# Three passes of a graph network kernel: rings of eight groups and resident indices in the score and harmonic passes, and TensorE's part of them as loops

## The chip, the cores and the metric

The kernel runs on one core of one Trainium2 chip. The metric is the device time of one launch in microseconds (us). The engines are called PE (TensorE, with its weight loads as PEld), DVE (VectorE), ACT (ScalarE), POOL (GpSimd) and SP (SyncE).

## What is computed

The reference is four graph layers on 12,500 nodes with 32 features and 200,000 edges, sorted by target node. Each layer adds its result to x. The parts that matter here, cut down:

```python
h = relu(layernorm(x)); x = x + gcn(h)          # three graph convolutions
h = relu(layernorm(x))                          # attention
q, k, v = h @ Wq, h @ Wk, h @ Wv
scores = einsum('ehd,ehd->eh', q[dst], k[src]) / sqrt(8)
e = exp(scores - segment_max(scores, dst)[dst])
x = x + (segment_sum(e * v[src], dst) / segment_sum(e, dst)) @ Wo
h = relu(layernorm(x)); x = x + relational(h)   # a gated sum over edges with 86 edge types
h = relu(layernorm(x))                          # spherical harmonics (9 numbers sh an edge)
x = x + segment_sum(W * cg * sh * h[src], dst)
```

## The kernel before

Edges are cut into steps of 128 edges, one to a partition, padded so that a step touches one tile of 128 nodes. There are S = 1664 steps. A group is G = 8 steps, so a pass has GROUPS = 208 groups; R = 4 and ITERS = 52 (4 x 52 = 208). Three passes are touched.

Each engine has its own program, and semaphores order them. In all three passes GpSimd gathers the rows of the source nodes from a table in HBM, one indirect DMA a step, eight a group, into a slot of a ring of R = 4 groups. It takes its row numbers from `staged`, into which VectorE copies the group's eight columns of the resident table `k["src"]` (`_stage`, L712). `_gather_rows` (L717, gathers recorded as L725) is the GpSimd program of the relation and harmonic passes; the score pass has its own copy of it (L1818). Before each group GpSimd waits for that group's index copy and for the slot to be free.

**Score pass** (`score_pass`, L1790). SP loads a group's target numbers as rows, broadcast over the partitions (L599). VectorE turns them into a transposed one-hot (`_one_hot_of_rows`, L604), one group ahead. TensorE multiplies the one-hot with the query table, eight matmuls a group (L1859), into `q_edge`, two groups deep in PSUM, which gives each edge its query. VectorE multiplies that with the gathered keys (L1840, two instructions a group), reduces to scores (L1845), and makes the index copy for the group three ahead (L714). SP copies the gathered slot to `dram["kv"]` for a later pass (L1873); it waits for the same gather as the product. A slot is free when the product has read it and the copy to `kv` has landed.

**Relation pass** (`relation_pass`, L2179). Works in half groups: VectorE makes three one-hots (L593, L604), then logits from looked-up rows, then the 2048-wide message (L2241). After the first half of each group it makes the index copy of the group three ahead. TensorE looks rows up (L2254, L2256) and adds messages into node tiles (L640). A one-hot of a half group waits for the look-up of the half after it and for earlier sums. At the end of the pass GpSimd gathers one more group and 98 tiles of `current`.

**Harmonic pass** (`harmonic_pass`, L2416). VectorE makes a group's one-hot (L593), copies its factors to PSUM (L2441), forms the messages (L2472, L2475) and makes the index copy. TensorE adds them into the node tile's sum (L640), and each matmul that ends a step counts `added` up. One-hot and message have two buffers: group n's one-hot waits until the sums of group n - 2 are counted. ScalarE takes finished tiles out (L668, L671).

In these three passes all programs except ScalarE's and the store of tiles are written out in full: the Python loops `for i in range(ITERS)` repeat the instructions 52 times. Elsewhere loops run on the engines (`Fori`): in the attention's value pass (`value_pass`, L2045), which reads `kv` back with plain DMAs and has no gathers, and in the three convolution sums, whose gathers are L1186, whose matmuls are L1261, and whose VectorE part starts with L1268.

## Time and profile before

| what | value |
|---|---|
| median of three runs | 18507.44 us |
| lowest and highest | 18477.56, 18517.64 us |
| span of the profiled execution | 18371.9 us |
| median above the profiled span | 135.5 us |
| GpSimd busy | 9678.5 us, 53% of the span |
| TensorE matmuls busy | 6824.2 us, 37% |
| VectorE busy | 6310.2 us, 34% |
| mean granted TensorE clock | 0.621 of full speed |

The profiled execution has no time of its own besides its span, so the table gives its distance to the median. Busy shares are averages over stages with different limits. The score pass runs from 8196 to 10600 us of the span, the relation pass from 11627 to 15240, the harmonic pass from 15605 to 18189. In the timelines a first number is the start, a second the length, and the brackets give the idle time of the engine before it and what the profile takes for its end; where the engine or transfer named there had long been done, it was another wait of the same instruction.

### The profile page before, as it was taken

How to read it: one execution, taken by the hardware profiler on the slowest of the kernel's cores; microseconds unless marked ns; L12 is line 12 of the kernel's file. 1: busy time of each engine (PE TensorE's matmuls, PEld its weight loads, DVE VectorE, ACT ScalarE, POOL GpSimd, SP SyncE). 2: the span in 40 equal slices, each digit the busy share in tenths (PEclk: the TensorE clock that was granted, in tenths of full speed). 3: DMA queues.
4: the chain of work that ended last, by engine and by line, in shares of the span. 5: the costliest groups of instructions: out<-in, count | busy, mean ns of one | idle time of the engine just before them, and what ended most of it. 6: DMA issues, size and time to landing. Idle time of an engine off the chain costs nothing. (4 is left out here: it accounts for less than half of the span.)

```text
span 18371.9 us, 155481 instructions
## 1 busy us (share of the span) xinstructions
PE 6824.2 (37%) x35336; PEld 4347.2 (24%) x35337; DVE 6310.2 (34%) x14818; ACT 2619.3 (14%) x4127; POOL 9678.5 (53%) x10318
## 2 busy tenths in 40 slices
PE   4122223444442122121111134566666666333335
PEld 1111112222221111110000023233333325333324
DVE  6222222222222333332222276455555541222222
ACT  1112223444442111110000000000000001000001
POOL 0566665555555666646666623344444441656663
PEclk9555555666665555555555555788888875666666
DMA  2111112222221111122222212222222222111111
GB/s 79 28 25 26 25 25 50 58 59 60 61 59 27 19 20 20 19 77 69 66 71 70 66 54 75 46 51 50 52 52 51 52 46 67 19 19 19 19 19 44
DMA packets 756927, 831.33 MB, mean 45 GB/s; under 512 B 348199, under 2 KB 521618, under 8 KB 753655
## 3 DMA queue, kind: packets, MB, share of 16 engines
q0 software_dynamic: 340624, 383.65, 11.4%
q1 hardware_dynamic: 267022, 300.82, 5.6%
q10 hardware_dynamic: 148312, 136.41, 2.7%
q8 instruction: 307, 5.03, 0.1%
q14 instruction: 662, 5.42, 0.1%
HBM read 658.55 MB, written 158.81 MB: 44 GB/s over the span
## 5 line engine op out<-in xcount | busy, mean ns | idle before, releaser
L725 POOL DMA_INDIRECT rel_ring<-scratch_tab,rel_staged x1664 | 1569.9, 943 | 1948.4 <-DVE rel_staged L714 1468.1
L640 PE MATMUL rel_accumulator<-rel_message,rel_onehot 128*128 128x512 f32 x3328 | 1998.0, 755 | 866.1 <-DVE rel_message L2241 818.7
L725 POOL DMA_INDIRECT sh_ring<-scratch_tab,sh_staged x1664 | 1569.8, 943 | 1318.6 <-DVE sh_staged L714 816.7
L1186 POOL DMA_INDIRECT sum1g_ring<-scratch_parts,sum1g_staged x1568 | 1548.3, 987 | 1163.4 <-SPq L1210 662.3
L1186 POOL DMA_INDIRECT sum0g_ring<-scratch_parts,sum0g_staged x1568 | 1539.8, 982 | 1166.3 <-issue 830.8
L1818 POOL DMA_INDIRECT score_ring<-scratch_tab,score_staged x1664 | 1571.9, 945 | 867.7 <-issue 516.9
L1186 POOL DMA_INDIRECT sum2g_ring<-scratch_parts,sum2g_staged x1568 | 1504.7, 960 | 945.8 <-issue 463.9
L640 PE MATMUL sh_accumulator<-sh_message,sh_onehot 128*128 128x248 f32 x3328 | 972.8, 461 | 1662.4 <-DVE sh_message L2475 1369.9
L640 PEld LDWEIGHTS sh_accumulator<-sh_message,sh_onehot 128*128 128x128 f32 x3328 | 788.9, 242 | 1845.7 <-issue 1726.1
L640 PEld LDWEIGHTS rel_accumulator<-rel_message,rel_onehot 128*128 128x128 f32 x3328 | 773.3, 245 | 1772.0 <-issue 1765.2
L1247 ACT COPY sum1g_rows<-sum1g_ring 128x6144 bf16 x196 | 1041.8, 5316 | 357.3 <-issue 315.8
L1859 PE MATMUL score_q_edge<-query_parts,score_onehot_t 128*128 x1664 | 256.4, 259 | 2158.0 <-DVE score_onehot_t L604 1453.5
L2241 DVE TENSOR_TENSOR rel_message<-numbers,rel_ring 128x2048 f32<-128x2048 f32 x416 | 953.3, 2292 | 14.3
L1261 PE MATMUL sum1g_totals<-sum1g_rows,sum1g_onehot 128*128 128x384 bf16 x3136 | 865.0, 456 | 195.9 <-ACT sum1g_rows L1247 155.7
L593 DVE TENSOR_TENSOR rel_onehot<-numbers,k_drel 128x512 f32<-128x512 f32 x419 | 288.2, 688 | 1761.8 <-DMA value_ring<-scratch_kv 1171.1
L593 DVE TENSOR_TENSOR sh_onehot<-numbers,k_drel 128x1024 f32<-128x1024 f32 x208 | 254.4, 1223 | 1801.1 <-DMA rlo_lin_chunk<-scratch_totals 1587.1
L1840 DVE TENSOR_TENSOR score_product<-score_q_edge,score_ring 128x384 f32<-128x384 f32 x416 | 212.2, 552 | 1883.2 <-DMA scratch_type_rows<-table_type_row 631.2
L1268 DVE TENSOR_REDUCE sum1g_joined<-sum1g_totals 128x128 f32<-128x384 f32 x196 | 109.3, 558 | 1969.5 <-remote 1302.2
L1859 PEld LDWEIGHTS score_q_edge<-query_parts,score_onehot_t 128*128 128x128 bf16 x1664 | 173.1, 104 | 2241.4 <-issue 2192.8
L1261 PE MATMUL sum0g_totals<-sum0g_rows,sum0g_onehot 128*128 128x98 bf16 x3136 | 308.2, 282 | 881.3 <-ACT sum0g_rows L1247 444.2
L1319 DVE TENSOR_TENSOR gcn_last<-gcn_last,sum0g_totals 128x2 f32 x196 | 30.1, 154 | 1725.6 <-remote 1536.2
L1261 PEld LDWEIGHTS sum1g_totals<-sum1g_rows,sum1g_onehot 128*128 128x128 bf16 x3136 | 497.4, 165 | 511.8 <-issue 469.2
(417 smaller groups left out, 12414.6 us busy)
## 6 DMA issues: line engine op xcount, KB each, us to landing
score_rows<-scratch_rel_rows SPq DMA_DIRECT2D x211, 256.0 KB
rel_rel_rows<-scratch_rel_rows ACTq DMA_DIRECT2D x211, 256.0 KB
scratch_kv<-score_ring SPq DMA_DIRECT2D x208, 256.0 KB
value_ring<-scratch_kv SPq DMA_DIRECT2D x208, 256.0 KB
rel_type_rows<-scratch_type_rows ACTq DMA_DIRECT2D x211, 172.0 KB
rel_ring<-scratch_tab,rel_staged POOLq DMA_INDIRECT x1672
score_ring<-scratch_tab,score_staged POOLq DMA_INDIRECT x1664
sh_ring<-scratch_tab,sh_staged POOLq DMA_INDIRECT x1664
```

Of the source, the lines that this page charges most:

```text
L593: return nc.vector.tensor_tensor(out[:], k["numbers"][:, 0:P].unsqueeze(1).to_broadcast([P, n, P]), k["drel"][:, bass.ds(first, n)].unsque ...
L640: self.nc.tensor.matmul(self.accumulator[:, bass.ds(self.banks[g], self.width)], onehot, rows, start=False, stop=True, skip_group_check=Tr ...
L725: nc.gpsimd.indirect_dma_start(out=ring[:, q, g, :], out_offset=None, in_=table, in_offset=bass.IndirectOffsetOnAxis(ap=staged[:, q, g:g + ...
L1186: nc.gpsimd.indirect_dma_start(out=ring[:, q % slots, g, :], out_offset=None, in_=table, in_offset=bass.IndirectOffsetOnAxis(ap=staged[:, ...
L1247: self.nc.scalar.copy(self.rows[q % 2][:, :, 0:3 * self.width], self.ring[:, bass.ds(slot, 1), :, :].rearrange("p o g w -> p (o g) w")).th ...
L1261: last = self.nc.tensor.matmul(self.totals[:, q % 2, 0:self.held], self.onehot[q % 2][:, :, g], self.rows[q % 2][:, g, :], start=(g == 0), ...
L1268: self.nc.vector.tensor_reduce(self.joined[q % 2][:], self.totals[:, q % 2, 0:3 * self.width].rearrange("p (c f) -> p f c", c=3), axis=AX_ ...
L1319: nc.vector.tensor_tensor(marks, marks, got.totals[:, q % 2, 3 * D:3 * D + 2], ALU.add)
L1818: nc.gpsimd.indirect_dma_start(out=ring[:, q, g, :], out_offset=None, in_=dram["tab64"][0:J * P, :], in_offset=bass.IndirectOffsetOnAxis(a ...
L1840: last = nc.vector.tensor_tensor(product[q % 2][:, tiles, :].rearrange("p g (c f) -> p g c f", f=D), q_edge[:, q % 2, b, 0:HALF_G * W].rea ...
L1859: last = nc.tensor.matmul(q_edge[:, q % 2, g // HALF_G, at:at + W], onehot_t[q % 2][:, g * P:(g + 1) * P], q_nodes[:, bass.ds(tiles[g] * W ...
L2241: nc.vector.tensor_tensor(message[m % 2][:].rearrange("p g (b f) -> p g b f", f=D), coef[:, m % 2, :, :].unsqueeze(3).to_broadcast([P, H, ...
```

## The change

1. `_stage` goes. Gathers of all three passes take their row numbers straight from `k["src"]`. GpSimd's program waits only for the slot (`slot_waits`); in the relation pass for `messaged`, and the extra group at its end waits for `messaged` too.
2. The rings of the score and harmonic passes have DEEP = 8 groups. The relation pass keeps four.
3. Score: three one-hots and three `q_edge` places instead of two. VectorE makes one-hots two groups ahead instead of one. SP loads rows four ahead.
4. Harmonic: four one-hots and four messages instead of two; group n's one-hot waits for the sums of group n - 4.
5. TensorE's programs of these two passes are loops: six groups a turn, 33 turns, with the first six and the last four groups written out (score); four groups a turn, 52 turns (harmonic). VectorE, GpSimd and SP stay written out.

```diff
-def _stage(nc, k, staged, group, slot):
-    return nc.vector.tensor_copy(staged[:, slot, :], k["src"][:, bass.ds(group * G, G)])
+def _gather_rows(nc, pool, k, table, ring, slots, gathered, slot_waits):
+    for n in range(GROUPS):
+        q = n % slots
+        slot_waits(n, q)
+        for g in range(G):
+            nc.gpsimd.indirect_dma_start(
+                out=ring[:, q, g, :], out_offset=None, in_=table,
+                in_offset=bass.IndirectOffsetOnAxis(ap=k["src"][:, n * G + g:n * G + g + 1], axis=0)).then_inc(gathered[q], DMA)
...
 def score_pass(nc, k, dram, q_nodes, score):
-        ring = sb("ring", [P, R, G, 2 * D])
+        ring = sb("ring", [P, DEEP, G, 2 * D])
-        onehot_t = [sb(f"onehot_t{h}", [P, G * P], BF16) for h in range(2)]
+        onehot_t = [sb(f"onehot_t{h}", [P, G * P], BF16) for h in range(3)]
-        q_edge = psum("q_edge", [P, 2, 2, BANK])
+        q_edge = psum("q_edge", [P, 3, 2, BANK])
+        def slot_waits(pool, n, q):
+            if n >= DEEP:
+                pool.wait_ge(used, n - DEEP + 1)
+                pool.wait_ge(spilled[q], n // DEEP * DMA)
+        def make_one_hot(dve, n):
+            dve.wait_ge(rowed[n % R], (n // R + 1) * DMA)
+            if n >= 3:
+                dve.wait_ge(looked_up, n - 2)
+            _one_hot_of_rows(nc, k, onehot_t[n % 3][:], rows[:, n % R, :]).then_inc(made, 1)
...
+                for n in range(GROUPS):
+                    if n + 2 < GROUPS:
+                        make_one_hot(dve, n + 2)
+                    dve.wait_ge(looked_up, n + 1)
+                    dve.wait_ge(gathered[n % DEEP], (n // DEEP + 1) * G * DMA)
...
             def _(pe):
+                def look_up(n, q):
+                    tiles = _tiles_of(nc, k, n)
+                    pe.wait_ge(made, n + 1)
+                    if not isinstance(n, int) or n >= 3:
+                        pe.wait_ge(used, n - 2)
...
+                for n in range(6):
+                    look_up(n, n)
+                with pe.Fori(0, GROUPS // 6 - 1) as i:
+                    for q in range(6):
+                        look_up(i * 6 + (q + 6), q)
+                for n in range(GROUPS // 6 * 6, GROUPS):
+                    look_up(n, n)
...
 def relation_pass(nc, k, dram, y_nodes, relations, current):
-                _gather_rows(nc, pool, dram["tab64"][0:J * P, :], staged, ring, indexed, released, gathered,
-                             lambda i, q: pool.wait_ge(messaged, (i * R + q) * 2 + 1))
-                pool.wait_ge(indexed, GROUPS + 1)
+                _gather_rows(nc, pool, k, dram["tab64"][0:J * P, :], ring, R, gathered,
+                             lambda n, q: pool.wait_ge(messaged, n * 2 + 1))
+                pool.wait_ge(messaged, GROUPS * 2 + 1)
...
 def harmonic_pass(nc, k, dram):
-        ring = sb("ring", [P, R, G, D])
+        ring = sb("ring", [P, DEEP, G, D])
-        onehot = [sb(f"onehot{h}", [P, G, P]) for h in range(2)]
-        message = [sb(f"message{h}", [P, G, SH_WIDTH]) for h in range(2)]
+        onehot = [sb(f"onehot{h}", [P, G, P]) for h in range(4)]
+        message = [sb(f"message{h}", [P, G, SH_WIDTH]) for h in range(4)]
+        def slot_waits(pool, n):
+            if n >= DEEP:
+                pool.wait_ge(messaged, n - DEEP + 1)
...
-                        dve.wait_ge(added, (i * R + q) * G + LEAD - G)
-                        _one_hot(nc, k, onehot[q % 2], (i * R + q) * G).then_inc(made, 1)
+                    if n >= 4:
+                        dve.wait_ge(added, (n - 3) * G + LEAD)
+                    _one_hot(nc, k, onehot[n % 4], n * G).then_inc(made, 1)
...
-                for i in range(ITERS):
-                    for q in range(R):
-                        adder = StepAdder(nc, pe, accumulator, SH_WIDTH, cleared, added, needed, _tiles_of(nc, k, i * R + q), _banks_of(nc, k, i * R + q))
+                with pe.Fori(0, GROUPS // 4) as i:
+                    for q in range(4):
+                        n = i * 4 + q
+                        adder = StepAdder(nc, pe, accumulator, SH_WIDTH, cleared, added, needed, _tiles_of(nc, k, n), _banks_of(nc, k, n))
```

`LEAD` is 25, and `added` starts at 25, so `(n - 3) * G + LEAD` is the count after the steps of group n - 4.

## Rows read from the trace of the kernel before

**Rows 1.** The page, part 5: the gathers of both passes; mean ns, then idle time before.

```profile
L725 POOL DMA_INDIRECT sh_ring<-scratch_tab,sh_staged x1664 | 1569.8, 943 | 1318.6 <-DVE sh_staged L714 816.7
...
L1818 POOL DMA_INDIRECT score_ring<-scratch_tab,score_staged x1664 | 1571.9, 945 | 867.7 <-issue 516.9
```

**Rows 2.** Busy time by stretch: length, engines' busy us (instructions), clock, DMA share, GB/s.

```profile
8196.00:10600.00 2404.00, 256.37 (x1664) 173.13 (x1664) 511.11 (x1040) 0.00 (x0) 1571.90 (x1664) 0.50 0.27 69
...
11627.00:15240.00 3613.00, 2362.81 (x13325) 1161.40 (x13326) 1781.41 (x3548) 198.44 (x612) 1669.94 (x1770) 0.79 0.25 50
15605.00:18189.00 2584.00, 972.19 (x3328) 788.93 (x3328) 753.16 (x1042) 74.96 (x201) 1569.84 (x1664) 0.68 0.10 19
```

**Rows 3.** Timeline of VectorE in the score pass: products; start, length, idle before.

```profile
9402.21 1.02 DVE L1840 TENSOR_TENSOR score_product<-score_q_edge,score_ring 128x384 f32<-128x384 f32 x2 [19.72 <-DMA scratch_sh<-table_sh]
...
9423.21 1.02 DVE L1840 TENSOR_TENSOR score_product<-score_q_edge,score_ring 128x384 f32<-128x384 f32 x2 [18.52 <-DMA table_tile<-scratch_rec,k_t_index]
...
9460.34 1.02 DVE L1840 TENSOR_TENSOR score_product<-score_q_edge,score_ring 128x384 f32<-128x384 f32 x2 [13.65 <-DMA scratch_type_rows<-table_type_row]
...
9462.73 1.02 DVE L1840 TENSOR_TENSOR score_product<-score_q_edge,score_ring 128x384 f32<-128x384 f32 x2
...
9598.94 1.02 DVE L1840 TENSOR_TENSOR score_product<-score_q_edge,score_ring 128x384 f32<-128x384 f32 x2 [15.03 <-DMA scratch_type_rows<-table_type_row]
```

**Rows 4.** Timelines of TensorE and of SP for the product at 9402.21.

```profile
9370.41 1.28 PE L1859 MATMUL score_q_edge<-query_parts,score_onehot_t 128*128 x8 [8.55 <-DVE score_onehot_t L604]
...
9387.72 0.34 SPq L1873 DMA_DIRECT2D scratch_kv<-score_ring  x1
```

**Rows 5.** Timeline of GpSimd in the score pass: one pause.

```profile
9435.47 0.94 POOL L1818 DMA_INDIRECT score_ring<-scratch_tab,score_staged  x1 [0.30 <-issue]
9447.52 0.94 POOL L1818 DMA_INDIRECT score_ring<-scratch_tab,score_staged  x1 [11.12 <-DVE score_staged L714]
```

**Rows 6.** Timeline of the harmonic pass: one cycle.

```profile
16922.57 1.23 DVE L593 TENSOR_TENSOR sh_onehot<-numbers,k_drel 128x1024 f32<-128x1024 f32 x1 [27.22 <-DMA rlo_lin_chunk<-scratch_totals]
...
16941.51 1.23 DVE L593 TENSOR_TENSOR sh_onehot<-numbers,k_drel 128x1024 f32<-128x1024 f32 x1 [5.53 <-DMA rlo_lin_chunk<-scratch_totals]
...
16945.39 6.60 PE L640 MATMUL sh_accumulator<-sh_message,sh_onehot 128*128 128x248 f32 x16 [5.55 <-DVE sh_message L2475]
...
16966.02 0.94 POOL L725 DMA_INDIRECT sh_ring<-scratch_tab,sh_staged  x1 [0.30 <-issue]
...
16972.35 1.22 DVE L593 TENSOR_TENSOR sh_onehot<-numbers,k_drel 128x1024 f32<-128x1024 f32 x1 [27.21 <-DMA rlo_lin_chunk<-scratch_totals]
...
16976.79 0.94 POOL L725 DMA_INDIRECT sh_ring<-scratch_tab,sh_staged  x1 [9.83 <-DVE sh_staged L714]
```

**Rows 7.** Waits of VectorE in the harmonic pass: total us, times, longest.

```profile
DVE sh_message L2472 <- DMA sh_ring<-scratch_tab,sh_staged: 19.3, 3, 10.0
```

**Rows 8.** Timeline of the relation pass: release and restart of one group.

```profile
13410.41 0.94 POOL L725 DMA_INDIRECT rel_ring<-scratch_tab,rel_staged  x1 [0.30 <-issue]
...
13413.17 0.69 DVE L593 TENSOR_TENSOR rel_onehot<-numbers,k_drel 128x512 f32<-128x512 f32 x1 [8.06 <-DMA value_ring<-scratch_kv]
...
13417.42 0.16 DVE L714 COPY rel_staged<-k_src 128x8 uint32<-128x8 uint32 x1
...
13418.41 0.94 POOL L725 DMA_INDIRECT rel_ring<-scratch_tab,rel_staged  x1 [7.06 <-DVE rel_staged L714]
```

**Rows 9.** Timeline of the second convolution sums, looped on TensorE.

```profile
5001.29 4.50 PE L1261 MATMUL sum1g_totals<-sum1g_rows,sum1g_onehot 128*128 128x384 bf16 x16
...
5011.92 0.95 POOL L1186 DMA_INDIRECT sum1g_ring<-scratch_parts,sum1g_staged  x1 [0.30 <-issue]
...
5019.29 0.56 DVE L1268 TENSOR_REDUCE sum1g_joined<-sum1g_totals 128x128 f32<-128x384 f32 x1 [17.37 <-remote]
```

**Rows 10.** Timeline of TensorE in the value pass: within a turn, and at one.

```profile
11207.39 1.41 PE L640 MATMUL value_accumulator<-value_parts,value_onehot 128*128 128x108 bf16 x8 [1.52 <-issue]
11210.71 1.42 PE L640 MATMUL value_accumulator<-value_parts,value_onehot 128*128 128x108 bf16 x8 [1.91 <-issue]
```

196 lines of the change are left out of this document (72 added, 124 removed).

## The prediction, on record before the change was built

> **What bounds the kernel now.** I read three views: the page, to see which engine is busiest; the stretches by stage, to see what the changed passes take; and the timelines of VectorE, TensorE and GpSimd inside each pass, to see which wait ends last.
>
> The page gives GpSimd the largest share, and the reader should see in its rows that a gather is 0.94 us of work [rows 1]. With the 0.30 us before each one [rows 6] a group of eight gathers costs 8 x 1.25 = 10.0 us, so 208 groups cost 2080 us. The stretches are longer [rows 2]: the score pass 2404 us (11.56 a group), the harmonic pass 2584 us (12.42), the relation pass 3613 us (17.4), while TensorE and VectorE are each busy for less than 40% of the first two. So no engine bounds these passes by its work. GpSimd's own floor is 324 us and 504 us below what they take, and something makes it pause.
>
> The timelines say what. In the score pass a product needs its gather and its look-up. For the product at 9402.21 [rows 3] the gather had landed when SP copied it out at 9387.72, and the eight matmuls had started at 9370.41 and were recorded done at 9371.69 [rows 4]. VectorE still waited until 9402.21, some 30 us after the matmuls, and the next product came 21.0 us later. At 9460.34 the wait is gone: products follow each other 2.4 us apart until VectorE is again limited by gathers. From 9460.34 to 9598.94, one such release to the next, lie 12 groups: 138.6 us, of which 120 are gathers and 19 are pauses of GpSimd (one of 11.1 us is shown [rows 5]). 208/12 x 19 = 329 us, which is the 324 us above the floor.
>
> I read this as TensorE's signals being held back while GpSimd issues gathers without a break, and cleared about 5 us after it stops. The harmonic pass shows it most plainly [rows 6]: the one-hot at 16972.35 waits for sums of a group that TensorE had finished before 16945.39; GpSimd's last gather ends at 16966.96; 5.4 us later VectorE is let go, and 4.4 us after that GpSimd starts again. The cycle from 16922.57 is 49.8 us for four groups: 40 of gathers and 9.8 of pause. VectorE waited for a gather only three times in the pass, 19.3 us in all [rows 7], so this ring was not short of rows. The relation pass has the same clock per group [rows 8]: the last gather starts at 13410.41, VectorE is let go at 13413.17, its index copy for GpSimd is at 13417.42, GpSimd starts at 13418.41; the copies are 16.7 us apart.
>
> Is it TensorE's written-out program? The sums of the first stage are loops on TensorE, and there too matmuls of 5001.29 (4.50 us) release VectorE only at 5019.29, 6.4 us after GpSimd's last gather of that run ended [rows 9]. So loops alone do not cure it.
>
> **The change part by part.** *Index copies removed.* 208 copies a pass of 0.16 us [rows 8] leave VectorE. In the score and harmonic passes one lies between VectorE's release and GpSimd's restart once a cycle: below 4 us. In the relation pass GpSimd now starts on the second half of a group's messages rather than on the copy after the first half of the next. Its period is 11.5 us (gather start to release) + 4.3 us (half a group on VectorE) + 0.9 us (copy and start); without the copy 0.15 us less, times 206 = 30 us. Moved starts could do more: if the look-up slips out before the hold, a half group of 4.3 us leaves the cycle in some groups (-250 us at 1.2 us a group); if instead two groups of gathers run together, the cycle for two is 21.5 us to the release, three half groups and the start, 35.3 us, or 17.6 each (+200 us). I take -30, since the release is still the end of the gathers.
>
> *Score: ring 4 to 8, buffers 2 to 3, one-hots two ahead.* Groups per cycle, checked on before: 2 outstanding ones clear at once, about 6 pass before the hold bites (some 30 us), and then one per 21 us: K = 2 + 6 + (10K - 30)/21, K = 12.5; 12 observed. After: 3 outstanding, and since VectorE now drains eight stored groups at 2.4 us I give 5.5 groups in 25 us: K = 3 + 5.5 + (10K - 25)/21, K = 14. The pause lies between 9 us (5.4 for clearing, one product, the restart) and the present 19; I take 13. That is 153/14 = 10.9 us a group, 2273 us: -131 us. Ends: nothing gained, or the floor (-324).
>
> *Harmonic: ring 4 to 8, one-hots and messages 2 to 4.* Before: 1 outstanding, 2 pass, then one per 31 us (the one-hots at 16941.51 and 16972.35 [rows 6]): K = 3 + (40 - 15)/31 = 3.8; 4 observed. After: of four groups in flight I count three as cleared at once (between one, as now, and four), K = 3 + 2 + (10K - 15)/31, K = 6.5 to 6.7. With the same 9.8 us pause, 74.8/6.5 = 11.5 us a group, 2392 us: -191 us. Ends: nothing, or the floor (-504). The eight slots themselves I cost at nothing, because gathers were late three times only.
>
> *TensorE as loops.* 33 turns of six groups and 52 of four. The value pass has a TensorE loop of four groups: its gap is 1.52 us between groups and 1.91 us at one of its turns [rows 10]. 85 x 0.39 = 33 us, hidden by TensorE's idle time (2148 us of the score pass, 1612 us of the harmonic one); without that cover 33 us. I take 0.
>
> The Trainium skill (Runtime: NRT & Kernel Launch, Instruction fetch mechanics) says that a taken branch whose target is outside the two pages held forces a fetch, and that kernels therefore prefer unrolling. The trace's loop of four groups does not show such a stall, so the sum keeps 0; by the rule it would be the fifth case below.
>
> Sum: -131 - 191 - 30 = -352 us on the profiled span of 18371.9, so 18020. The median of the runs is 135.5 us above that span and I carry the difference: 18507 - 352 = 18155.
>
> **The rivals.** *Floor reached.* If deeper buffers carry VectorE over the held signals, or the hold leaves with TensorE's long program, both passes run at 10.0 us a group: -324 - 504 - 30 = -858, 17,650. For it: the floor is where GpSimd is plainly full. Against it: while gathers run, a score group is signalled each 21 us, and no finite buffer makes that 10; and the looped sums have the hold too.
>
> *Nothing moves.* Between two pauses TensorE may get a fixed amount of signalling through. Then more room adds no groups per cycle: 12 and 4 stay, and only the copies go: about 18,470. For it: in the harmonic pass the ring was not what was short. Against it: four buffers leave more to be cleared in each pause.
>
> *Slower: the clearing grows with what is outstanding.* Its place is the pause: 5.4 us clears about one harmonic group now; if three take three times as long, the pause is near 21 us, and with the restart 25. Harmonic (65 + 25)/6.5 = 13.8, +295 us; score (140 + 25)/14 = 11.8, +47 us; less 30: about 18,820. It decides from pauses of 15.7 us (harmonic, 6.5 x 2.42) and 21.8 us (score, 14 x 1.56). For it: the harmonic release, with more matmuls behind it, shows how long clearing takes and not what it depends on. Against it, in the score pass: at 9460.34 two groups cleared within 2.4 us.
>
> *The loops cost a fetch a turn.* At the whole gap of a turn in the value pass, 1.91 us, on the path each time: 85 x 1.91 = 162 us back, 18,317. Named above as the skill's rule; the trace speaks against it.
>
> **How the numbers follow.** Forecast 0.52, floor 0.18, nothing moves 0.14, slower 0.12, fetch 0.04. The forecast's own range is 17,950 to 18,350 (K from 5 to 8 and from 12 to 18). The range for 8 in 10 runs from the floor to a little above no change, 17,650 to 18,560, which leaves out the slower case and the tails. About 0.2% (37 us) is what the measurement can tell from nothing. Faster: 0.52 + 0.18 + 0.04 + a third of 0.14 = 0.79. Within: half of 0.14 = 0.07. Slower: the rest, 0.14.
>
> **What would show it.** In the profile after: score near 2270 us and harmonic near 2390, both with GpSimd's runs longer (14 and 6 to 7 groups) and pauses of 10 to 13 us; product starts 21 us apart late in each run; the relation pass within 30 us or so of 3583 and its period still 16.5; the gather still 0.94 + 0.30. The prediction is wrong if GpSimd never pauses, if the runs stay at 12 and 4 groups, if pauses pass 16 us, or if the relation pass moves by more than 100 us.

## The result, and the profile after

The kernel after takes 18221.89 us (median of 4 runs, 18196.34 to 18284.28) beside 18492.5 us for the kernel before in the same job (4 runs): 0.9857 of its time, 95% interval 0.9834 to 0.988, so about 271 us faster. The forecast was 352 us faster. The profiled execution is 18194.7 us long, 177 us less than that of before; its start of the score pass comes 32 us later, in stages that the change does not touch.

The stretches of the three passes after, in the columns of [rows 2]:

```profile
8228.00:10600.00 2372.00, 334.87 (x1664) 173.23 (x1664) 504.00 (x830) 0.00 (x0) 1573.26 (x1664) 0.50 0.27 69
11626.00:15162.00 3536.00, 2246.73 (x13384) 1098.68 (x13384) 1798.58 (x3340) 206.75 (x624) 1669.77 (x1770) 0.82 0.25 51
...
15514.00:18015.00 2501.00, 1108.41 (x3328) 755.55 (x3328) 729.36 (x833) 77.21 (x206) 1569.94 (x1664) 0.62 0.11 19
```

Against [rows 2] the score pass lost 32 us (forecast 131), the harmonic pass 83 us (forecast 191), and the relation pass 77 us by these windows (forecast 30). VectorE's 208 index copies per pass are gone from the instruction counts.

Two cautions. The windows of [rows 2] end 14 us and 4 us before the relation and harmonic passes of before do (ScalarE's last copy there ends at 15254.5 and 18191.8); to the same mark these passes lost 91 and 86 us. And the profile of before is not of one of the four runs beside the kernel after: in the runs on record a time is 1.7 us above its own span (18196.34 and 18194.7), while 18371.9 us lies 101 us below the fastest of those four (18473.06). It fits the runs of before in the later jobs (18344.7 to 18366.79 us, see below). Against the later profiles of the same three programs before's score pass is 36 to 40 us longer, its relation pass 113 to 125 us and its harmonic pass 86 to 93 us. These falls add up to about 250 us and are the better measure.

VectorE's timeline in the score pass answers to [rows 3]:

```profile
9451.37 1.02 DVE L1832 TENSOR_TENSOR score_product<-score_q_edge,score_ring 128x384 f32<-128x384 f32 x2 [11.58 <-DMA k_x<-in_x]
9453.77 1.00 DVE L1832 TENSOR_TENSOR score_product<-score_q_edge,score_ring 128x384 f32<-128x384 f32 x2
...
9461.27 1.00 DVE L1832 TENSOR_TENSOR score_product<-score_q_edge,score_ring 128x384 f32<-128x384 f32 x2
...
9467.57 1.02 DVE L1832 TENSOR_TENSOR score_product<-score_q_edge,score_ring 128x384 f32<-128x384 f32 x2 [3.73 <-issue]
...
9488.61 1.02 DVE L1832 TENSOR_TENSOR score_product<-score_q_edge,score_ring 128x384 f32<-128x384 f32 x2 [18.53 <-issue]
...
9511.00 1.02 DVE L1832 TENSOR_TENSOR score_product<-score_q_edge,score_ring 128x384 f32<-128x384 f32 x2 [19.99 <-DMA k_x<-in_x]
...
9553.03 1.02 DVE L1832 TENSOR_TENSOR score_product<-score_q_edge,score_ring 128x384 f32<-128x384 f32 x2 [17.13 <-DMA k_x<-in_x]
```

The reader should see three things. Five products run 2.4 to 2.5 us apart, the sixth is 6.3 us behind, then the steps are 21 to 22.4 us, and the last is 19.6. The stretch at 10 us, in which before was limited by gathers, is missing. And from one release (9451.37) to the next (9553.03) lie 101.7 us with nine groups, 11.3 us each, not the fourteen of the forecast. (The releaser named, a transfer long done, is not the one: the wait is for the look-up.) GpSimd's timeline shows what it waits for:

```profile
9534.70 0.94 POOL L718 DMA_INDIRECT score_ring<-scratch_tab,k_src  x1 [2.37 <-DVE score_product L1832]
...
9554.32 0.94 POOL L718 DMA_INDIRECT score_ring<-scratch_tab,k_src  x1 [9.94 <-DVE score_product L1832]
```

Both pauses end with a product, the one that frees the slot eight groups back: the ring of eight is full when GpSimd stops. TensorE's timeline between the same products shows what "held back" looks like in its own records:

```profile
9492.82 0.24 PE L1850 MATMUL score_q_edge<-query_parts,score_onehot_t 128*128 x1 [1.85 <-issue]
9494.22 0.24 PE L1850 MATMUL score_q_edge<-query_parts,score_onehot_t 128*128 x1 [1.16 <-issue]
...
9497.02 0.24 PE L1850 MATMUL score_q_edge<-query_parts,score_onehot_t 128*128 x1 [1.09 <-issue]
9498.42 0.24 PE L1850 MATMUL score_q_edge<-query_parts,score_onehot_t 128*128 x1 [1.16 <-issue]
```

Matmuls of 0.24 us start mostly 1.40 us apart (some 0.7 us), waiting for nothing that the profile names, and 6 to 10 us pass between the eight of one group and the eight of the next. So in this timeline the matmuls are recorded late, not only their signals; the run with fixed addresses below shows that these records have to be read with care.

The harmonic pass, one cycle, beside [rows 6]:

```profile
16894.95 1.23 DVE L593 TENSOR_TENSOR sh_onehot<-numbers,k_drel 128x1024 f32<-128x1024 f32 x1 [37.12 <-DMA rlo_lin_chunk<-scratch_totals]
16898.42 1.22 DVE L593 TENSOR_TENSOR sh_onehot<-numbers,k_drel 128x1024 f32<-128x1024 f32 x1
...
16905.35 1.21 DVE L593 TENSOR_TENSOR sh_onehot<-numbers,k_drel 128x1024 f32<-128x1024 f32 x1
16928.52 1.23 DVE L593 TENSOR_TENSOR sh_onehot<-numbers,k_drel 128x1024 f32<-128x1024 f32 x1 [19.64 <-issue]
16955.25 1.22 DVE L593 TENSOR_TENSOR sh_onehot<-numbers,k_drel 128x1024 f32<-128x1024 f32 x1 [23.17 <-DMA rlo_lin_chunk<-scratch_totals]
...
16959.08 0.94 POOL L718 DMA_INDIRECT sh_ring<-scratch_tab,k_src  x1 [10.67 <-DVE sh_message L2467]
```

Four one-hots come 3.5 us apart where one came before, and the cycle, 16894.95 to 16955.25, is 60.3 us for five groups instead of 49.8 for four. The pause is 10.7 us. In the relation pass, beside [rows 8]:

```profile
13426.76 0.69 DVE L593 TENSOR_TENSOR rel_onehot<-numbers,k_drel 128x512 f32<-128x512 f32 x1 [7.45 <-PE rel_accumulator L640]
...
13428.80 2.29 DVE L2236 TENSOR_TENSOR rel_message<-numbers,rel_ring 128x2048 f32<-128x2048 f32 x1
...
13431.36 0.94 POOL L718 DMA_INDIRECT rel_ring<-scratch_tab,k_src  x1 [6.53 <-DVE rel_message L2236]
```

GpSimd starts 4.6 us after VectorE's release (13426.76); before it was 5.2 us. What was saved is the restart itself. These rows of before and, last, one of after show the work that came before GpSimd's restart:

```profile
9444.21 1.02 DVE L1840 TENSOR_TENSOR score_product<-score_q_edge,score_ring 128x384 f32<-128x384 f32 x2 [18.52 <-DMA scratch_type_rows<-table_type_row]
...
9446.53 0.17 DVE L714 COPY score_staged<-k_src 128x8 uint32<-128x8 uint32 x1
```

```profile
13415.21 2.29 DVE L2241 TENSOR_TENSOR rel_message<-numbers,rel_ring 128x2048 f32<-128x2048 f32 x1
```

```profile
16974.76 1.15 DVE L2475 TENSOR_TENSOR sh_message<-sh_factors,sh_ring 128x960 f32<-128x960 f32 x1
```

```profile
16957.66 1.15 DVE L2467 TENSOR_TENSOR sh_message<-sh_factors,sh_ring 128x960 f32<-128x960 f32 x1
```

After, GpSimd starts 0.27 us after the end of the product or message that frees its slot, in all three passes (score 9554.05 to 9554.32, relation 13431.09 to 13431.36, harmonic 16958.81 to 16959.08). Before, it started 2.29 us after it in the score pass (9445.23 to 9447.52), where a reduction and a one-hot ran ahead of the index copy, 0.91 us in the relation pass (13417.50 to 13418.41) and 0.88 us in the harmonic pass (16975.91 to 16976.79).

### The profile page after: what moved, and what is told of

Its sections match the earlier page's. It is cut to its first block and busy times, and to the rows that moved or that the text cites. A ratio compares the mean times of both kernels' runs of the same rounds, so it can differ in the third digit from the quotient of the medians.

```text
span 18194.7 us, 155378 instructions
## 1 busy us (share of the span) xinstructions
PE 6911.0 (38%) x35336; PEld 4249.0 (23%) x35337; DVE 6289.4 (35%) x14183; ACT 2623.4 (14%) x4127; POOL 9698.7 (53%) x10318
## 3 DMA queue, kind: packets, MB, share of 16 engines
q0 software_dynamic: 340624, 383.65, 11.5%
## 5 line engine op out<-in xcount | busy, mean ns | idle before, releaser
L718 POOL DMA_INDIRECT rel_ring<-scratch_tab,k_src x1664 | 1569.7, 943 | 1848.9 <-DVE rel_message L2236 1332.8
L640 PE MATMUL rel_accumulator<-rel_message,rel_onehot 128*128 128x512 f32 x3328 | 1930.5, 733 | 1097.1 <-DVE rel_message L2236 734.0
L718 POOL DMA_INDIRECT sh_ring<-scratch_tab,k_src x1664 | 1569.9, 943 | 1213.3 <-issue 497.8
L718 POOL DMA_INDIRECT score_ring<-scratch_tab,k_src x1664 | 1573.5, 946 | 811.6 <-issue 494.4
L640 PE MATMUL sh_accumulator<-sh_message,sh_onehot 128*128 128x248 f32 x3328 | 1108.4, 466 | 1440.3 <-issue 1346.3
L1850 PE MATMUL score_q_edge<-query_parts,score_onehot_t 128*128 x1664 | 334.9, 249 | 2060.5 <-issue 1679.3
```

What stands on the lines that cost most here:

```text
L640: self.nc.tensor.matmul(self.accumulator[:, bass.ds(self.banks[g], self.width)], onehot, rows, start=False, stop=True, skip_group_check=Tr ...
L718: nc.gpsimd.indirect_dma_start(out=ring[:, q, g, :], out_offset=None, in_=table, in_offset=bass.IndirectOffsetOnAxis(ap=k["src"][:, n * G ...
L1850: last = nc.tensor.matmul(q_edge[:, q % 3, g // HALF_G, at:at + W], onehot_t[q % 3][:, g * P:(g + 1) * P], q_nodes[:, bass.ds(tiles[g] * W ...
```

## The experiments

The kernel before took 18344.7 to 18366.79 us in their jobs, less than beside the kernel after, and the same relation pass took 3502 to 3514 us beside 3536: 0.6 to 1.0% of difference between jobs that is no effect of an edit. So times are compared by ratio or by the difference to before in the same job (271 us for the kernel after), and passes among the experiments. A pass is a stretch of the profiled execution. e6 looks up fixed tiles and e7 fetches fixed rows, so these two leave out the choice of rows and don't compute the reference.

| run | median us | before in the job | ratio (95%) | score | relation | harmonic |
|---|---|---|---|---|---|---|
| e1_written_out | 18115.32 | 18365.79 | 0.9861 (0.9832 to 0.9891) | 2363 | 3511 | 2486 |
| e2_resident_only | 18189.68 | 18365.79 | 0.99 (0.9871 to 0.9928) | 2354 | 3508 | 2554 |
| e3_ring4 | 18104.53 | 18365.79 | 0.9846 (0.9816 to 0.9877) | 2359 | 3505 | 2489 |
| e4_two_buffers | 18206.84 | 18365.79 | 0.9916 (0.9883 to 0.995) | 2375 | 3509 | 2569 |
| e5_lookups_twice | 18109.78 (1 run) | 18366.79 | | 2381 | 3502 | 2497 |
| e6_fixed_addresses | 18147.58 (1 run) | 18366.79 | | 2354 | 3504 | 2499 |
| e7_score_plain_dma | 16612.59 (1 run) | 18366.79 | | 843 | 3506 | 2501 |
| e8_relation_bursts | 18123.84 | 18366.79 | 0.9866 (0.9849 to 0.9882) | 2364 | 3505 | 2496 |
| e9_relation_ahead | 18023.79 | 18344.7 | 0.9821 (0.9795 to 0.9847) | 2368 | 3394 | 2499 |
| e10_gaps_in_score | 18231.57 (1 run) | 18344.7 | | 2488 | 3508 | 2494 |
| e11_harmonic_six | 18084.39 | 18344.7 | 0.9851 (0.983 to 0.9873) | 2357 | 3514 | 2483 |
| f2_gaps_by_halves | 17757.42 | 18352.9 | 0.9668 (0.9651 to 0.9684) | 2360 | 3179 | 2455 |

**Which part of the change did it.** Four kernels, each with one part undone or alone.

The loops undone:

```diff
-                with pe.Fori(0, GROUPS // 6 - 1) as i:
...
+                for n in range(6, GROUPS):
+                    look_up(n, n)
...
-                with pe.Fori(0, GROUPS // 4) as i:
+                for i in range(GROUPS // 4):
```

> The changed kernel with TensorE's programs of the score and harmonic passes written out again. Two theories. Buffers: the gain of these two passes comes from the deeper one-hot and message buffers, so they stay at 2372 and 2501 us (within 15), and the late steps of a score cycle stay near 22 us. Program: loops free TensorE's signals, so writing the program out brings both back to 2405 and 2588 us or above. In between: if each instruction of TensorE is charged while gathers run, leaving out the loop's register instructions makes the late score step 21.0 instead of 22.4 us, and both passes shorter by 10 to 40 us.

Only the resident indices, on the kernel before (its rings of four, its buffers, its written-out programs; the copies of indices gone in all three passes):

```diff
-            pool.wait_ge(indexed, i * R + q + 1)
...
-                    in_offset=bass.IndirectOffsetOnAxis(ap=staged[:, q, g:g + 1], axis=0)).then_inc(gathered[q], DMA)
+                    in_offset=bass.IndirectOffsetOnAxis(ap=k["src"][:, n * G + g:n * G + g + 1], axis=0)).then_inc(gathered[q], DMA)
```

> The kernel before with one part of the change: row numbers taken from the resident table in all three passes, no index copies; rings, buffers and written-out programs as before. If the relation pass gains by the earlier and copy-free restart of GpSimd alone, it takes 3536 us as in the changed kernel (from 3628), and score and harmonic stay within 20 us of 2405 and 2588. If the gain needs something else, the relation pass stays above 3600. Whole kernel 80 to 120 us faster by the first, within 30 us by the second.

The rings back to four:

```diff
-DEEP = 8
+DEEP = 4
```

> The changed kernel with rings of four groups instead of eight. By the forecast's theory (stored groups let a longer run of gathers go on) score loses its gain and goes to 2405 or above, harmonic by a few us. By the rival (a run of gathers ends when TensorE's signals have used up what gets through between two pauses) the ring's depth only shifts the stock: score within 15 us of 2372, harmonic within 15 of 2501.

Two buffers again, rings of eight kept:

```diff
-                    if n + 2 < GROUPS:
-                        make_one_hot(dve, n + 2)
+                    if n + 1 < GROUPS:
+                        make_one_hot(dve, n + 1)
...
-        onehot = [sb(f"onehot{h}", [P, G, P]) for h in range(4)]
-        message = [sb(f"message{h}", [P, G, SH_WIDTH]) for h in range(4)]
+        onehot = [sb(f"onehot{h}", [P, G, P]) for h in range(2)]
+        message = [sb(f"message{h}", [P, G, SH_WIDTH]) for h in range(2)]
```

> The changed kernel with two one-hots and two q_edge places made one group ahead (score) and two one-hots and messages (harmonic), rings of eight kept. If what clears at a pause is the number of outstanding groups, harmonic goes back to four groups a cycle of 49.8 us, 2588 us, and score to about 2400. If the ring of eight is what gives the gain, both stay at 2501 and 2372.

The harmonic stretches of e4_two_buffers and, after it, e3_ring4:

```profile
15479.00:18048.00 2569.00, 969.82 (x3328) 787.80 (x3328) 735.16 (x833) 76.69 (x205) 1571.25 (x1664) 0.68 0.10 19
```

```profile
15486.00:17975.00 2489.00, 1101.80 (x3328) 749.18 (x3328) 729.33 (x833) 77.05 (x206) 1571.44 (x1664) 0.62 0.11 19
```

The indices alone give 176 us of the 251 to 261 us that e1 and e3 give in that job: beside the profile of before the relation pass falls by 119 us, the score pass by 50 and the harmonic pass by 33. e2's own expectation had only the relation pass right; it kept the other two within 20 us. The buffers give 65 to 80 us in the harmonic pass (2554 and 2569 with two, in e2 and e4, against 2489 with four). In the score pass they give nothing over the indices: with two buffers it takes 2354 us in e2 and 2375 in e4, with three 2357 to 2372 us. The ring of eight gives nothing: a ring of four is not slower in any pass. Nor do the loops: written out, the score and harmonic passes take 2363 and 2486 us, and the late steps of the score pass stay at 22.4 us in e1. With ring, loops and indices but two buffers (e4) the kernel is no faster than with the indices alone.

The quicker restart accounts for what the indices give, by an estimate from the rows above and GpSimd's waits before: 203 stops of the relation pass at 0.64 us are 130 us, 54 of the harmonic pass at 0.61 us are 33 us, and 36 of the score pass at 2.02 us are 73 us, beside 119, 33 and 50 measured.

**What holds TensorE.** The look-ups of the score pass done twice:

```diff
-                    for g in range(G):
+                    for g in list(range(G)) * 2:
```

> One look. In the score pass every one of TensorE's eight look-up products of a group is done twice, on the same operands into the same place. If what GpSimd's gathers slow down is each single instruction of TensorE (theory), the products of VectorE inside a stretch of gathers come not 22 us apart but some 38 us (the group grows from about 26 to 42 instructions of TensorE, at 0.85 us each), and the pass grows by more than 200 us. If TensorE's work is done in time and only the signal at the end of a group is held (rival), the step stays at 22 us and the pass within 30 us of 2372.

```profile
9163.79 1.02 DVE L1832 TENSOR_TENSOR score_product<-score_q_edge,score_ring 128x384 f32<-128x384 f32 x2 [32.44 <-DMA k_x<-in_x]
...
9171.18 1.00 DVE L1832 TENSOR_TENSOR score_product<-score_q_edge,score_ring 128x384 f32<-128x384 f32 x2
9184.07 1.02 DVE L1832 TENSOR_TENSOR score_product<-score_q_edge,score_ring 128x384 f32<-128x384 f32 x2 [10.31 <-DMA k_x<-in_x]
9220.46 1.02 DVE L1832 TENSOR_TENSOR score_product<-score_q_edge,score_ring 128x384 f32<-128x384 f32 x2 [33.99 <-DMA k_x<-in_x]
```

In these timelines of VectorE the last step is 36.4 us, and the first groups of the pass came 44.8 and 42.7 us apart, twice 22.4; in the rest of the pass the long steps are 36 to 38 us. So the price grows with the number of matmuls, and a signal held only at the end of a group is ruled out. Yet the pass took 2381 us, 17 us more than in e8, whose score pass is that of the kernel after: the theory was right on the step and wrong on what it costs. In this cycle five groups pass from release to release in 56.7 us, 11.3 each as before; over the pass GpSimd stops 51 times for 306 us, in the kernel after 41 times for 280 us.

Fixed addresses:

```diff
-                                                q_nodes[:, bass.ds(tiles[g] * W - W, W)], start=True, stop=True)
+                                                q_nodes[:, g * W:g * W + W], start=True, stop=True)
```

> One look. The score pass looks up at fixed tiles: TensorE loads no registers and computes no addresses there (the values looked up are not the reference's). Theory that all of TensorE's instructions count, those on registers too: 16 instead of 26 a group, so the step inside a stretch of gathers falls from 22 us to about 13.5 us and the pass falls below 2280 us. Rival, that only matmuls and weight loads count: the step stays at 22 us. Rival, that the reads of the addresses from memory are the whole of it: the step falls under 10 us and the pass comes to its floor of 2080 us.

TensorE's timeline there:

```profile
9397.09 0.82 PE L1849 MATMUL score_q_edge<-query_parts,score_onehot_t 128*128 128x96 bf16 x8 [21.58 <-issue]
9419.57 0.82 PE L1849 MATMUL score_q_edge<-query_parts,score_onehot_t 128*128 128x96 bf16 x8 [21.65 <-issue]
```

The steps of TensorE and of VectorE's products are still 22.4 us, the first rival's: instructions on registers don't count (the pass fell by 10 us beside e8), 22.4 us / 8 = 2.8 us for each pair of weight load and matmul does. Without them between, the records bunch eight matmuls into 0.82 us, some 19 us before the next product starts. Why the same step shows spread matmuls in one kernel and bunched ones in another, no run shows; I go by the step from group to group and not by a record's place within it.

Plain transfers instead of gathers:

```diff
-            @block.gpsimd
-            def _(pool):
-                _gather_rows(nc, pool, k, dram["tab64"][0:J * P, :], ring, DEEP, gathered, lambda n, q: slot_waits(pool, n, q))
+            @block.scalar
+            def _(act):
...
+                        act.dma_start(ring[:, q, g, :], dram["tab64"][t * P:(t + 1) * P, :]).then_inc(gathered[q], DMA)
```

> One look. The score pass fetches its rows with plain transfers of fixed tiles, eight a group as before and of the same size, put out by ScalarE; GpSimd does nothing in that pass (the values are not the reference's). Theory, that GpSimd's gathers are what slows TensorE's signals: no product is 10 us or more behind the one before, and the pass takes under 1400 us. Rival, that the transfers themselves or the pass's waits on other engines make the steps: steps of 15 to 22 us remain and the pass takes over 2000 us.

```profile
8197.00:9040.00 843.00, 254.10 (x1664) 173.18 (x1664) 487.17 (x830) 0.00 (x0) 0.00 (x0) 0.50 0.69 193
```

4.05 us a group, at nearly three times the traffic per second (193 GB/s against 69), and no product more than 5.8 us behind the last: GpSimd's gathers slow TensorE, not the traffic. The Trainium skill (DMA: Bandwidth & Descriptors, SWDGE vs HWDGE vs iDMA) says that GpSimd computes each descriptor of its transfers in software and writes it to rings in SBUF, and that transfers issued by ScalarE don't pass there. The trace agrees as far as that the second kind leaves TensorE alone (843 us); that the writing of descriptors is the cause, no run here shows.

**Can the pauses be arranged better?** Each four gathers of the relation pass wait for their own half slot:

```diff
-                             lambda n, q: pool.wait_ge(messaged, n * 2 + 1))
...
+                        if g % H == 0:
+                            pool.wait_ge(messaged, max(n * 2 + g // H, 1))
```

> The relation pass's GpSimd waits before each four gathers, not before each eight, for the half of its ring slot: two bursts of 5 us a group instead of one of 10. Theory, that TensorE is slowed only once gathers have run for about 5 us and is free again some 5 us after they stop: a group takes 13 to 15 us instead of 16.2, so the kernel is 250 to 600 us faster than the kernel after. Rival, that each stop costs its own 5 us of clearing: two pauses of 6.5 us a group, 23 us, and the kernel over 1000 us slower. Rival, that the gathers of the second half were never ahead: 16.2 us and no difference within 40 us.

```profile
13409.13 0.94 POOL L2287 DMA_INDIRECT rel_ring<-scratch_tab,k_src  x1 [6.36 <-DVE rel_message L2236]
13425.20 0.94 POOL L2287 DMA_INDIRECT rel_ring<-scratch_tab,k_src  x1 [6.39 <-DVE rel_message L2236]
```

GpSimd's timeline shows one pause in 16.1 us still: the two halves come 4.4 us apart, so when one burst ends the next is free. The last rival holds.

More room ahead in the relation pass, and in the harmonic pass:

```diff
-        message = [sb(f"message{m}", [P, H, WIDTH]) for m in range(2)]
+        message = [sb(f"message{m}", [P, H, WIDTH]) for m in range(4)]
-        looked = psum("looked", [P, 2, BANK])
+        looked = psum("looked", [P, 4, BANK])
-                            dve.wait_ge(added, n * H + LEAD - H)
+                            dve.wait_ge(added, n * H + LEAD - 3 * H)
...
-                            look_up(pe, n + 3, m + 3, ahead[q + 1 + h][(1 - h) * H:(2 - h) * H])
+                            look_up(pe, n + 4, m + 4, ahead[q + 2][h * H:(h + 1) * H])
```

> The relation pass gets four message buffers instead of two and looks up four half groups ahead instead of three, through four PSUM banks instead of two. Theory that what ends each of GpSimd's 6.4 us pauses is VectorE working off one half group after a late signal of TensorE, as in the harmonic pass before: more half groups pass in one pause, a group takes 13 to 14.5 us instead of 16.1, and the kernel is 350 to 650 us faster than the kernel after. Rival, that TensorE's own work of a group must all be done between the stop of the gathers and some 8 us after they go on, whatever VectorE may do ahead: the pauses get rarer and longer in proportion, and the pass stays within 60 us of 3505 to 3535 us.

```diff
-        onehot = [sb(f"onehot{h}", [P, G, P]) for h in range(4)]
-        message = [sb(f"message{h}", [P, G, SH_WIDTH]) for h in range(4)]
+        onehot = [sb(f"onehot{h}", [P, G, P]) for h in range(6)]
+        message = [sb(f"message{h}", [P, G, SH_WIDTH]) for h in range(6)]
...
-                    if n >= 4:
-                        dve.wait_ge(added, (n - 3) * G + LEAD)
+                    if n >= 6:
+                        dve.wait_ge(added, (n - 5) * G + LEAD)
```

> The harmonic pass gets six one-hots and six messages instead of four, both rings have four groups, and TensorE's program of the harmonic pass is written out. Theory that each further buffer lets one more group pass in a pause of the same length (two buffers: 4 groups a pause, 12.2 us each; four: 5 groups, 11.95): 6 to 7 groups a pause, 11.5 to 11.75 us each, a pass of 2390 to 2445 us. Rival, that the pause grows with the groups that pass in it: within 20 us of the 2489 us that the pass took with rings of four.

Both fell short. The relation pass took 3394 us, 111 us less than in e8, between the 60 us of the rival and the 350 of the theory. The harmonic pass took 2483 us, 3 to 6 us less than with four buffers (2486 in e1, 2489 in e3), the size that its rival has; but the pauses did not get longer and rarer as the rival says. GpSimd stops 49 times for 386 us in it, in e3 46 times for 378 us, so here more buffers change nothing.

**Gaps.** What no part of the forecast allowed came from a run meant to measure how long a gap must be:

```diff
+                        if g % 4 == 3:
+                            if n + g > 3:
+                                pool.wait_ge(padded, n * 2 + g // 4)
+                            nc.gpsimd.tensor_copy(pad[:], k["iota"][:].unsqueeze(1).to_broadcast([P, 8, P])).then_inc(padded, 1)
```

> One look. In the score pass GpSimd copies a 128x1024 block into a spare tile after each four gathers, a gap of some 2 to 2.5 us that does no work of the reference. Theory that only gathers back to back for longer than about 8 us slow TensorE: no products 20 us apart any more, a steady 14 to 15.5 us a group and a pass of 2950 to 3250 us. Rival, that a gap must last over 5 us to clear TensorE: stretches with products 20 us or more apart stay, and the pass takes over 3250 us, gaps and pauses together.

```profile
9405.27 0.94 POOL L1821 DMA_INDIRECT score_ring<-scratch_tab,k_src  x1 [0.30 <-issue]
9406.21 1.05 POOL L1827 COPY score_pad<-k_iota 128x1024 f32<-128x1024 f32 x1
9407.43 0.97 POOL L1821 DMA_INDIRECT score_ring<-scratch_tab,k_src  x1 [0.17 <-issue]
...
9407.81 1.02 DVE L1842 TENSOR_TENSOR score_product<-score_q_edge,score_ring 128x384 f32<-128x384 f32 x2 [9.59 <-issue]
...
9410.37 1.22 PE L1860 MATMUL score_q_edge<-query_parts,score_onehot_t 128*128 x8 [10.81 <-DVE score_onehot_t L604]
...
9419.77 1.02 DVE L1842 TENSOR_TENSOR score_product<-score_q_edge,score_ring 128x384 f32<-128x384 f32 x2 [9.56 <-issue]
```

Some 1.2 us without a gather after each four, and the score pass is steady: 12.0 us from product to product (9407.81 to 9419.77), gathers and copies on end, no pause and in the whole pass no step over 12.2 us. Each product follows the landing of its own gathers: SP's copy of the slot, which waits for the same gathers, starts at 9407.75. The theory holds in what it says of the steps; its 14 to 15.5 us a group and 2950 us or more were missed, since the gap came out at half of what was expected. It also shows that the gathers' transfers alone don't slow TensorE, since the same ones move here at 66 GB/s. For this pass 12.0 us is worse than 11.4. For the relation pass, at 16.1 us, it would be better; the last kernel tried six kinds of stretch.

```diff
+        each, width = gap(n)
...
+            if g % each == each - 1:
+                if copies:
+                    pool.wait_ge(padded, copies)
+                nc.gpsimd.tensor_copy(pad[:, 0:width, :], k["iota"][:].unsqueeze(1).to_broadcast([P, width, P])).then_inc(padded, 1)
+                copies += 1
...
+                             lambda n: (4, 2) if n < GROUPS // 2 else (8, 8))
...
+                             lambda n: (4, 8) if n < GROUPS // 2 else (4, 4))
...
+                             lambda n: (4, 4) if n < GROUPS // 2 else (8, 8))
```

> The kernel after with GpSimd copies into a spare tile between its gathers, in six kinds of stretch, each half of a pass. Relation: 128x1024 after each four gathers, then 128x512 after each four. Score: 128x256 after each four, then 128x1024 after each eight. Harmonic: 128x512 after each four, then 128x1024 after each eight. Theory, from the 1.04 us that a 128x1024 copy took and the steady 12.0 us a group with one after each four gathers: where a gap suffices, a group takes 10 us and its copies and is steady (relation 12.0 and 11.0; score 10.5 and 11.0; harmonic 11.0 and 11.0), in all about 1140 us less than the kernel after, with the relation pass alone down from 3505 to 2400 us. Rival A, that a burst of eight gathers (10 us) is too long: the second halves of score and harmonic show steps of 20 us and more and take 11.5 to 13.5 us a group; some 900 us less. Rival B, that a copy of 0.3 to 0.6 us is too short: steps of 20 us and more where the copy is 128x256 or 128x512; the relation pass then takes 2400 to 3200 us. Rival C, that TensorE and VectorE can't do the relation pass's group in 12 us at all, their work being 9 to 10 us with waits on each other: 13 to 15 us a group there with regular pauses.

The copies (count, busy us, mean ns of one), and the relation pass's messages of the first and the second half (count, shortest, median and longest ns, first and last start):

```profile
L726 POOL COPY rel_pad<-k_iota 128x1024 f32<-128x1024 f32 x208 | 217.5, 1046 | 0.9
L726 POOL COPY rel_pad<-k_iota 128x512 f32<-128x512 f32 x208 | 129.1, 620 | 1.0
...
L726 POOL COPY score_pad<-k_iota 128x1024 f32<-128x1024 f32 x104 | 108.8, 1046 | 0.4
...
L726 POOL COPY score_pad<-k_iota 128x256 f32<-128x256 f32 x208 | 85.2, 410 | 21.5 <-remote 17.8 <-issue 2.5
```

```profile
L2246 DVE TENSOR_TENSOR rel_message<-numbers,rel_ring x208: 2290/2291/2293, 11609.0 to 13025.2; 128x2048 f32<-128x2048 f32 x104
```

```profile
L2246 DVE TENSOR_TENSOR rel_message<-numbers,rel_ring x209: 2290/2291/2292, 13025.2 to 14752.9; 128x2048 f32<-128x2048 f32 x105
```

To read a gap's worth from half a pass one has to know how the two halves differ without it. In e8, which has no gaps, the same rows are:

```profile
L2236 DVE TENSOR_TENSOR rel_message<-numbers,rel_ring x208: 2291/2291/2293, 11639.0 to 13296.1; 128x2048 f32<-128x2048 f32 x104
```

```profile
L2236 DVE TENSOR_TENSOR rel_message<-numbers,rel_ring x208: 2290/2291/2293, 13300.6 to 15081.3; 128x2048 f32<-128x2048 f32 x104
```

A group has two messages. In e8 the first 104 groups of the relation pass take (13300.6 - 11639.0) / 104 = 16.0 us each and the others 17.2 us, so the halves are not alike. Worked out likewise for each half of each pass, from the starts of the products or messages:

| pass, half | us a group without gaps (e8) | gap | us a group with it (f2) |
|---|---|---|---|
| relation, first | 15.98 | 1.05 us after each four | 13.66 |
| relation, second | 17.21 | 0.62 us after each four | 16.65 |
| score, first | 12.02 | 0.41 us after each four | 11.56 |
| score, second | 10.71 | 1.05 us after each eight | 11.13 |
| harmonic, first | 12.56 | 0.62 us after each four | 12.03 |
| harmonic, second | 11.28 | 1.05 us after each eight | 11.42 |

How far runs of one and the same program differ in a half bounds what can be read from this. The kernel after, e8 and e9 have the same score pass and differ by 0.3 us in its halves (11.75 to 12.02 and 10.71 to 11.05); the harmonic pass (after, e8, e10) differs by 0.14 us at most and the relation pass (e1, e8, e10) by 0.06. So the gap of 1.05 us after each four gathers is worth 2.3 us a group of the relation pass, and 0.62 us after each four is worth 0.5 to 0.6 us there. In the harmonic pass, 41 us shorter in all than in e8 (2455 against 2496), 0.62 us after each four is worth perhaps 0.5 us. A gap of 1.05 us after each eight shows no gain, and neither does the score pass as a whole (2360 us with gaps, 2364 without).

Rival B holds for the short copies: in the first halves of score and harmonic 26 and 19 steps of 20 us and more stay (34 and 24 in e8), and the relation pass takes 3179 us. Rival A holds in its steps (21 and 29 stay in the second halves), while the 11.1 and 11.4 us a group lie just under its 11.5. Rival C holds in the relation pass, which takes 13.7 us a group at the long gap and is not steady at 12.0: GpSimd still stops there. The kernel takes 17757.42 us, 0.9668 of before, the fastest of those that leave nothing of the work out. With the long gap in the second half of the relation pass too, another (2.32 - 0.56) x 104 = 183 us might go, an estimate from this table that takes the gain of the first half for the second; it was not run.

## Why the prediction was right or wrong

The direction, the range and the forecast's own range (17,950 to 18,350) hold. The working behind them holds in part, and that the sum came near is partly luck: the buffers were priced at 322 us and give 65 to 80, the index copies at 30 us and give 176, and the two errors offset each other. Of the signs named, the runs didn't stay at 12 and 4 groups (nine and five in the cycles above, for 14 and 6 to 7), the pauses in them stayed under 16 us (the longest wait of the harmonic pass is 18.6 us) and the gather at 0.94 + 0.30 us; the relation pass, by the better measure, moved by more than the 100 us named as a sign of being wrong. The 135.5 us carried from span to median are a difference between two executions of before and no cost of a launch; they don't touch the 352 us.

*The reading.* That GpSimd's floor is 10.0 us a group and that its pauses make up the rest is right (e10, which has no pauses, is gathers and copies alone). That TensorE is held while gathers run back to back is right, and e7 shows it from the other side. "Signals being held back" was too narrow: twice the matmuls took 36 to 45 us instead of 22 (e5), which a signal held at a group's end would not do.

*Index copies, -30.* Mis-sized. They are the largest part of the change: 176 us in e2. The restart lost 0.6 us in the relation and harmonic passes and 2.0 us in the score pass, and not the 0.15 us of the copy: GpSimd started 0.8 us after the copy's end before and starts 0.27 us after the message or product now, and in the score pass the copy also stood behind a reduction and a one-hot. I had priced the instruction instead of the step that it was in the chain from release to restart, and had put the score and harmonic passes at "below 4 us" (50 and 33 measured). Why GpSimd took 0.8 us after the copy, no run separates: the change took a wait and a semaphore increment out of its program together, and gave it another tile to read the row numbers from.

*Score, -131, measured 0 beyond the indices.* The pass fell by 32 to 40 us, and the indices alone (e2) took off 50. The step that failed is "K = 14": one cycle has nine groups. The estimate let products outstanding be added to what passes in the gathers' time. In fact GpSimd stops when the ring is full; after a release it gets as many slots as products pass, and eight slots are as full in the steady state as four. What counts is how many groups pass per us of pause, and that is the same with ring four or eight, with two or three buffers within 21 us, and with twice the matmuls within 17 us. Why it is the same, no run shows.

*Harmonic, -191, measured -83 to -93, of which the indices are 33 and the buffers 65 to 80.* The mechanism was right, the size off: five groups pass in a 60.3 us cycle, where the forecast had 6.5 in 74.8. Of four groups in flight three were to be cleared at once beside two more that pass; four one-hots came 3.5 us apart in all. Six buffers (e11) give 3 to 6 us more. The eight slots at nothing were right.

*Loops, 0.* Right (e1). The rule of the Trainium skill (Runtime: NRT & Kernel Launch, Instruction fetch mechanics), that kernels prefer unrolling since taken branches may force a fetch, is not seen here: written out, the two passes changed by 1 and 10 us from e8. Whether the turns of these loops leave what is held, no run here shows.

*The rivals.* "Nothing moves" missed the total (18,470), since it had the copies at 30 us too; it was nearest to the truth on the score pass, where a number of groups per pause does not grow with room. "Slower" did not come: the harmonic pause grew from 9.8 to 10.7 us and not to 25. "Floor reached" failed for the reason given.

*What stays open.* Why a weight load and a matmul cost 2.8 us while GpSimd gathers, why it is free for several microseconds after gathers resume, and why a gap of 1.2 us undoes more than its share. The runs bound it: not registers, not the traffic, not the length of TensorE's program. Gaps longer than 1.05 us, and gaps in the three sums of the first stage, which have the same hold [rows 9], were not tried.

## What to carry to other kernels

When a ring's producer pauses, ask first whether the ring is full: deeper rings do nothing for a loop that always runs full, while taking one step out of the way from release to restart pays each time. Price such a step by the time between the end of the work that frees the slot and the restart, not by the length of the instruction. When one engine slows another, look for a small rest in the first before buffering the second: 1.05 us of idle copying after each four gathers was worth 2.3 us a group in half of the relation pass (241 us), more than all of the change's buffers. Try such a rest per pass, since the same copy costs 0.6 us a group net in the score pass. And before reading an effect from half of a pass, read the same half of a run without it: here the halves differ by 1.2 us a group by themselves.

## What the runs showed of the hardware that I had not expected

- While GpSimd issues gathers 1.25 us apart, a group of eight look-ups on TensorE takes 22.4 us (2.8 us for each pair of weight load and matmul), and sixteen take 36 to 45 us (e5); the matmuls of 0.24 us are recorded mostly 1.40 us apart in one kernel and eight together in 0.82 us in another (e6).
- Leaving out the address computation on TensorE's registers leaves the step at 22.4 us (e6).
- 1.2 us without a gather after each four removes the long steps in the score pass (12.0 us, steady, e10) and takes the first half of the relation pass from 16.0 to 13.7 us a group; a copy of 0.62 us after each four takes its second half from 17.2 to 16.65.
- The same bytes by plain transfers from ScalarE's queue let the score pass run at 4.05 us a group.
- GpSimd starts its next gather 0.27 us after the VectorE instruction that frees the slot ends, in the rows of all three passes, and started 0.8 us after the end of an index copy before.
